# Exps over slots of two and four PSUM banks in turn, a ring of nine pexp places, and later experts' weights held back

## The reference, cut to what matters

```python
# attention (per batch b, head h)
q, k = rms_norm(q), rms_norm(k)
attn = softmax(einsum('bhnd,bhmd->bhnm', q, k) * scale)
y = einsum('bhnm,bhmd->bhnd', attn, v)
y = y - sum(y * Vn) * Vn          # Vn: v over its norm
x = x + (y, heads joined) @ w_proj.T
# state-space stage gives cond2(x); then, per expert e of 8
mask = (argmax(route) == e)
out = out + mask * (gelu(h @ W1[e]) @ W2[e])
x = x + out * max_prob
```

## Time and profile before

| | |
|---|---|
| median of 3 runs | 846.78 us (845.64 to 847.67) |
| the profiled execution | 847.82 us |
| its span, first to last instruction | 846.1 us |
| mean granted TensorE clock | 0.983 of full |
| PE busy | 782.2 us (92%) |
| ACT busy | 526.1 us (62%) |
| DVE busy | 460.7 us (54%) |
| L872, the exps: 256 instructions | 237.8 us |
| L1725, the values | 138.8 us |
| L1713, the scores | 96.8 us |
| w_all DMAs | 16 of 1024 KB |

### The profile page before, as it was taken

The page is one execution under the profiler, slowest core; times in us unless marked ns, Lnnn a source line. Parts: engine busy times, 40 slices in busy tenths (PEclk is TensorE's granted clock), DMA queues, the critical chain, the costliest instruction groups (busy, mean ns, idle before and its releaser), DMA issues.

```text
span 846.1 us, 13449 instructions
## 1 busy us (share of the span) xinstructions
PE 782.2 (92%) x4456; PEld 511.0 (60%) x4456; DVE 460.7 (54%) x828; ACT 526.1 (62%) x699; POOL 248.0 (29%) x308
## 2 busy tenths in 40 slices
PE   8999999998999999888999999998799699999995
PEld 5778888887777875233222222223645488888884
DVE  4887666388766641533201202112447479999994
ACT  4432222463232237978999999997445188888883
POOL 5434444134434305100000001000000347777762
PEclk9999999999999999799999999999999799999998
DMA  9131111001243045064551353100189621111000
GB/s 249 18 77 51 50 50 50 26 25 49 77 149 100 1 67 84 0 117 167 67 76 32 44 74 53 21 0 0 50 304 379 238 83 49 52 51 52 26 11 0
DMA packets 52674, 64.87 MB, mean 77 GB/s; under 512 B 15889, under 2 KB 43929, under 8 KB 52636
## 3 DMA queue, kind: packets, MB, share of 16 engines
q1 hardware_dynamic: 44564, 55.96, 26.1%
q0 software_dynamic: 3312, 6.31, 2.4%
q10 hardware_dynamic: 4760, 2.12, 0.9%
HBM read 51.52 MB, written 15.60 MB: 79 GB/s over the span
## 4 chain that ended last, share of the span: by engine, by line
PE 66%; ACT 12%; DVE 9%; issue 8%; DMA 3%; ACTq 0%; SPq 0%; POOLq 0%; DVEq 0%
PE psum L1573 44%; ACT pexp L872 9%; PE psum L1725 8%; PE psum L1713 4%; PE psum L1929 2%; DMA x_d<-x_tm 2%; PE psum L1843 1%; DVE hl L1021 1%; DVE hh L1170 1%; PE psum L1779 1%; DMA x_tm<-in_x 1%; DVE yT L1269 1%; PE psum L1676 1%; PE psum L1829 1%; DVE ssum L1210 1%
## 5 line engine op out<-in xcount | busy, mean ns | idle before, releaser
L872 ACT ACTIVATE pexp<-psum 128x1024 f32<-128x1024 f32 x256 | 237.8, 1086 | 15.4 <-PE psum L1713 15.4
L799 ACT ACTIVATE hid<-psum,b_col 128x512 f32<-128x512 f32 x96 | 66.0, 689 | 160.8 <-PE psum L1573 107.6
L1725 PE MATMUL psum<-pexp,v_ones 128*32 128x512 f32 x1024 | 138.8, 615 | 18.4 <-ACT pexp L872 11.6
L1713 PEld LDWEIGHTS psum<-q_stack,k_stack 48*128 48x128 f32 x512 | 39.7, 188 | 111.9 <-ACT pexp L872 94.3
L1170 DVE TENSOR_SCALAR hh<-hid,scale_col 128x341 fp32r<-128x341 f32 x192 | 69.3, 402 | 69.7 <-ACT hid L799 52.8
L1713 PE MATMUL psum<-q_stack,k_stack 48*128 48x512 f32 x512 | 96.8, 453 | 7.2 <-DVE parts L1263 3.5
L1021 DVE SCALAR_TENSOR_TENSOR hl<-hid,scale_col,hh 128x341 fp32r<-128x341 f32 x192 | 96.3, 543 | 3.4
L1573 PE MATMUL psum<-hh,w2h 128*128 128x512 f32 x192 | 76.4, 398 | 3.4 <-DVE hl L1021 3.2
L1573 PE MATMUL psum<-x_hi,w1h 128*128 128x512 f32 x192 | 77.0, 401 | 0.7 <-DVE x_lo L1035 0.6
L1573 PE MATMUL psum<-hh,w2l 128*128 128x512 f32 x192 | 75.0, 391 | 0.0
L1573 PE MATMUL psum<-x_hi,w1l 128*128 128x512 f32 x192 | 74.9, 390 | 0.0
(11 more groups left out here) (277 smaller groups left out, 1477.9 us busy)
## 6 DMA issues: line engine op xcount, KB each, us to landing
w_all<-in_L_ffn_W SPq DMA_DIRECT2D x16, 1024.0 KB, 13.7
raw<-in_L_cond_ew SPq DMA_DIRECT2D x32, 256.0 KB, 3.3
parts_d<-parts SPq DMA_DIRECT2D x8, 1024.0 KB, 5.0
q_stack<-parts_d SPq DMA_DIRECT2D x48, 128.0 KB, 4.7
k_stack<-parts_d SPq DMA_DIRECT2D x48, 128.0 KB, 7.6
raw<-in_L_cond_sw SPq DMA_DIRECT2D x16, 256.0 KB, 3.3
x_d<-x_tm SPq DMA_DIRECT2D x2, 1024.0 KB, 5.0
x_d<-x_tm ACTq DMA_DIRECT2D x4, 512.0 KB, 11.8
```

The source lines that it names most:

```text
L799: act.activation(hid[k % 4][:], bank(k % 4), ACT.Gelu_apprx_tanh, bias=b1_col[:, bass.ds(4 * q + k // 2, 1)]).then_inc(gelu_done, 1)
L872: act.activation(pexp[mt % 2][:, 2 * j:2 * j + 2, 512 * h:512 * h + 512], psum[:, 2 * r:2 * r + 2, :], ACT.Exp, scale=D ** -0.5)\
L1713: ins = pe.matmul(psum[:, 2 * r + lane, :], k_stack[i][rows, j, mt * P:(mt + 1) * P], q_stack[i][rows, j, 512 * h:512 * h + 512], start=Tr ...
L1725: ins = pe.matmul(psum[VW * j:VW * j + VW, 6 + h, :], v_ones[i][:, mt, j, :], pexp[mt % 2][:, j, 512 * h:512 * h + 512], start=(mt == 0), ...
```

## The change

Four things change in attention, and two in the feed-forward stage.

- **Slots.** Banks 0 to 5 are now a slot of two banks (4 and 5) and a slot of four (0 to 3). A group is a list of cycles (cycles): one unit into the two-bank slot, then two units into the four-bank slot. ACT takes one exp of 128x1024 for the first and one of 128x2048 for the other two. A group of the loop has 11 cycles, 22 exps.
- **Holes.** A cycle of which the turned yT or a turn_b takes banks 2 and 3 has only one unit in the four-bank slot (holes): cycle 5 in the groups of the loop, cycles 3, 5, 7 and 10 in group 1 (12 cycles), cycle 10 in group 0. The turn is issued behind that cycle's scores; the next cycle's four-bank scores wait until DVE has read banks 2 and 3.
- **Ring.** pexp is one buffer with nine places of a unit each (place); the ninth lets units 7 and 8 lie side by side for one exp. x and qk buffers and yT lie elsewhere in SBUF.
- **Values.** The 16 calls are no longer one behind every second unit. Each cycle has two places for a call: behind the two-bank scores and behind the four-bank scores (values_at). The last two of a group are done in cycle 0 of the next. In a loop group the cycles 0, 2, 4, 7 and 9 have both calls, cycle 6 has only the first and 1, 3, 5, 8 and 10 only the second.
- **Weights.** SP waits for x3_stored ahead of expert 4, so experts 4 to 7 are loaded behind the stores of x3.
- **x_lo_part.** DVE splits tile 0's tokens ahead of the weights of tile 1, no longer behind them.

```diff
+        def cycles(g):
+            hole, out, u = holes(g), [], 0
+            while u < UNITS:
+                four = [u + 1] if len(out) in hole else [u + 1, u + 2]
+                out.append((u, four, hole.get(len(out))))
+                u += 1 + len(four)
...
             for e in range(spare, RE - under_route):
+                if e == 4:
+                    sp.wait_ge(x3_stored, 16 * 2 * NB)
                 load_expert(e)
...
+            def exp_units(g, units, banks):
+                act.wait_ge(scored, UNITS * g + units[-1] + 1)
+                for u in units:
+                    if u % HG == 0:
+                        after(act, av_done, LT * g + u // HG - 1)
+                n, p = len(units), place(units[0])
+                act.activation(pexp[:, p:p + n, :, :].rearrange("p u l n -> p (u l) n"),
+                               psum[:, banks:banks + 2 * n, :], ACT.Exp, scale=D ** -0.5).then_inc(exp_done, 1)
...
+                for c, (two, four, _) in enumerate(cycles(g)):
+                    exp_units(g, [two], 4)
+                    exp_units(g, four, 0)
...
             w1_lo_parts(0, RE - 1)
             dve.wait_ge(x3_stored, 16 * 2 * NB)
+            x_lo_part(0, 0)
             w1_lo_parts(1, place_of_expert(dve, 1))
-            x_lo_part(0, 0)
             x_lo_part(1, 1)
...
+                for c, (two, four, next_hole) in enumerate(cycles(g)):
+                    after(pe, exp_done, base + 2 * c - 1)
+                    scores(i, two, 4)
+                    give_values(c, 0)
+                    after(pe, exp_done, base + 2 * c)
+                    if hole and hole[0] == "qk":
+                        pe.wait_ge(part_lo, 8 + hole[1] + 1)
+                    elif hole:
+                        pe.wait_ge(y_read, g)
+                    for n, u in enumerate(four):
+                        scores(i, u, 2 * n)
+                    if next_hole and next_hole[0] == "qk":
+                        turn_b(next_hole[1])
+                    elif next_hole:
+                        turn(g - 1)
+                    hole = next_hole
+                    give_values(c, 1)
```

## The result

| | before | after |
|---|---|---|
| median of the runs timed side by side | 847.22 us (845.64 to 850.54) | 859.88 us (857.92 to 865.92) |
| the profiled execution | 847.82 us | 860.92 us |
| its span | 846.1 us | 859.2 us |
| start of the first exp | 328.5 us | 330.0 us |
| first exp's start to last exp's end | 256.2 us | 271.7 us |

The changed kernel is slower: ratio 1.0158, 95% interval 1.0129 to 1.0186. Executions in a slower state of the chip, with a mean granted clock of 0.84 for instance, are left out of every time and ratio here. In the profiled executions the 13.1 us split into +1.5 ahead of attention, +15.5 in the exps and -4.0 behind them. The prediction had +12.4 in the exps, -0.9 at attention's end and -8.4 for the weights. So both parts went the way it said, attention lost more and the weights gave less.

The account below looks back on a forecast made before the run. The prediction took ACT to bound attention's loop. For the profiled execution it summed 847.82 + 11.5 (attention) - 8.4 (weights) = 850.9 us, or 849.9 against the median (+3.1 us), range 841 to 856.

Parts of the forecast that it names:

- The exps themselves: ACT in attention: an exp of 2048 lasts 1.88 us; a merged pair saves 0.05, 4 us in eight groups.
- The four-bank slot as a loop of its own: Attention: exp plus hand-overs and two units take 2.71 to 2.77 us a cycle, against ACT's own need of 2.68.
- The two-call cycles and the turn: PE in loop groups: two-call cycles 2.99 us, the turn's 3.68; a group 32.0 against 30.5, +9.0 for six groups.
- Group 1: Attention's group 1, where turn_b holds half of the large slot: 38.5 to 38.7 us against 35.6, +3.0.
- Group 0: Attention: group 0's turn_b delays group 1's first cycle and costs a unit in its own; +0.4 us.
- The end of attention: The first of the last two calls of values can go one exp earlier: -0.9 us.
- The held-back weights: Feed-forward start: x3 stored sooner, tokens 6.4 us earlier, kept full clock 2.0 more; -8.4 us, between -5 and -9.
- Later loads hidden: Feed-forward: experts 4 to 7 land near 662, 670, 677 and 684, ahead of need, so their later loading costs nothing.
- (b): Rival: the weights pay less, gathers held up by loads or expert_up waiting for w1b_lo; -5, 853.3 us; chance 0.15.
- (a): Rival: ACT keeps its pace and bounds the loop; attention between 0 and +5, 841.4 us with +3; chance 0.22.
- (c): Rival: both parts are smaller, attention +8.5 and weights -8; 847.3 us, no change; chance 0.2.
- (d): Rival: the clock falls in attention as PE's busy share drops from 0.93 to some 0.86; 865 us and more; chance 0.05.

Follow-up runs that it names:

- slots_only: The changed kernel without SP's wait for x3_stored and with the old order of x_lo_part: 861.55 us, ratio 1.0165.
- the paced profiles: The kernel before with loads of experts 4 to 7 set out between the gathers: 840.13 us; with x_lo_part moved 840.5; with an earlier last call but one 839.6.
- weights_behind_gathers: The kernel before with experts 4 to 7 all loaded behind tokens_known and the first three gathers: 841.75 us, ratio 0.993.
- the version with narrow calls: The changed kernel with some calls of values made on 128 of their 512 columns, leaving out part of the sums: 855.0 us, ratio 1.0085.
- weights_only: The kernel before with only SP's wait for x3_stored ahead of expert 4 and x_lo_part(0, 0) first: 843.21 us, ratio 0.9949.

## Why the prediction was wrong, by its own steps

It said 849.9, slower at 0.54, range 841 to 856. The time is 859.88: the sign of the likeliest case was right, the size was not, and the time lies outside the range. The 10.0 us that the profiled execution is above the sum of 850.9 divide so: 3.1 in the exps, 5.3 behind them, 1.5 ahead of them. Two steps failed: the price of a unit of scores, and the price of a gather beside the loads with the kept clock that hung on it.

- **The exps themselves**: an exp of 2048 lasts 1.88 us, as worked out. The saving of 0.05 us a pair never came to bear, since ACT waits ahead of most of them. So this part of the prediction, and the 93 ns of the Trainium skill's page "ScalarE: Activation LUTs" (section What ACT_TABLE_LOAD costs) beside it, decided nothing.
- **The four-bank slot as a loop of its own**: right, and it is the cause. One-call cycles take 2.70 to 2.79, where 2.71 to 2.77 was predicted, and with single exps the loss is gone (30.7 against 32.6 a group).
- **The two-call cycles and the turn**: the mechanism was right, **the term of a unit of scores was mis-sized**. It took 0.33, half of the 0.66 of two units side by side. A unit alone between two calls costs 0.43, and the new order of calls has such single units where the old one had pairs. A two-call cycle is 3.08, not 2.99, the turn's 3.87, not 3.68: 4 x 0.09 + 0.19 = 0.55 a group, and 32.0 became 32.6. The chain of waits of the kernel before had shown single units:

```profile
383.56 0.42 PE psum L1713
...
385.45 0.99 PE psum L1725 x8
...
393.64 0.43 PE psum L1713
```

  The prediction read only a stretch where two stood together, and divided. In the groups' lengths, groups 2 to 7 lost 12.1 us where 9.0 - 0.9 were due.
- **Group 1**: 38.44, within 0.2 of the prediction; +2.8 for the +3.0.
- **Group 0**: +0.4 predicted; the two profiled executions differ by -0.2. A spell of lower clock behind the square root comes and goes (37.7 to 40.3 us from the first exp to the first copy of yT, over both orders), so it isn't settled.
- **The end of attention**: -0.9 predicted, -0.87 measured by the last copy of yT. In the profiled execution it didn't reach tokens_known: from the last exp's end to there it took 73.4 us, against 73.2 before. In `slots_only` it took 72.2, so the saving is real; the profiled execution lost 1.1 us again on the way, with the clock granted at 0.85 and 0.72 from 657 to 665.
- **The held-back weights**: **the step that failed most is "I take 0.3 more" for the gather beside the loads.** It measured 6.25 us, 3.3 above its 2.98, beyond even the upper end of 3 more. The second failure hangs on it: PE ran out of work, the clock fell, and of the 2.0 us for the kept clock only 0.6 came (6.05 us from the first turn to the first matmul of tile 1, against 6.65). So the gather missed by 3.0 us and the clock by 1.4; with the 1.1 of the item above these are the 5.3. The 2.0 would not have been safe with a quick gather either, as the paced profiles show. The stores at 3.0 to 4.1 us and the start of the gather were right. The arbitration by packets, for which the prediction named the Trainium skill's page "DMA: Bandwidth & Descriptors" (section Queues, rings and completion order), had been used to place the gather near the lower end. No run contradicts that rule: of the loads issued ahead of the gather, the fourth landed 9.8 us after the gather's issue, and the gather itself after 6.25. What didn't follow from it is that a gather beside full queues is cheap.
- **Later loads hidden**: right in the changed kernel, where PE waits for no gather behind the first. But in `weights_behind_gathers` the transfers of the late loads did hold up tile 4's gather, which the prediction didn't ask about.
- **x_lo_part**: nothing, as said.
- **The rivals**: (b), weights pay less, was the one that came true, and beyond its bound: -3.1 against its -5 in the profiled execution. (a) and (c) fell with the two-call cycles. (d), the clock falls in attention, didn't happen in the changed kernel's loop groups, but did in the version with narrow calls. Its premise, that the clock fell before only behind a far longer wait, was wrong: in the kernel before it was granted at 0.59 from 620 to 624, where the wait just ahead of it was 1.36 us.
- **Ahead of attention**: the first exp starts between 328.0 and 330.5 us over all profiled executions of all versions, whose instructions are the same up to there. A row of the changed kernel's chain of waits, where the kernel before took 3.02 us for twelve such matmuls:

```profile
195.04 4.59 PE psum L1611 x12
```

  `weights_only` has the same 4.59, and its code is that of the kernel before up to there. So these 1.5 us are the clock's in one execution, and no part of the change.

The range already had both worst terms at once in its upper end: 846.78 + 15 - 5 = 856.8, where it said 856. It failed because the weights' term was bounded too tightly, and because it left nothing for the execution. In the profiled one attention came to 15.5 - 0.9 = +14.6, inside its +15, but the weights gave -3.1, and 1.5 us came from ahead of attention.

## What to carry to other kernels

Merging instructions of the engine that bounds a stage frees no time when the merged one also holds the buffers that the other engine must refill: count, for the slot, the consumer's duration plus everything the producer does in order before it comes back to that slot, and compare it with the bound before. Take the price of a short instruction from a row in which it stands between the same neighbours as it will, not as half of a pair. When large transfers are moved out of the way of one small critical transfer, look where they land: the next small transfer on the path can pay the same price, so set them out between the small ones.

## What the runs showed of the hardware

- The first gather of 128 rows took 2.97 to 3.52 us with few other transfers or none (DMA share 0.13 to 0.20 while it ran, eight profiles), and 6.25 to 6.49 us beside the loads of experts 4 to 6 (share 1.06 to 1.07, five profiles); tile 4's took 6.69 in `weights_behind_gathers`.
- A store of 512 KB took 3.0 to 4.1 us with no loads queued, 8.9 to 15.1 behind them.
- A pair of score matmuls alone between two calls costs PE 0.43 us, two pairs in a row 0.66, three 0.89.
- TensorE's clock stayed at 1.00 in attention's two windows of the changed kernel with PE busy 17.7 of 20 us, and fell to 0.54 in one stretch of the version with narrow calls, behind 8.1 of 10. In the kernel before it stayed at 1.00 with PE busy 14.5 of 20 us, so the busy share alone doesn't tell when it falls.
